# Two accumulators in place of three for the experts' rows, in a block of attention and 64 routed experts

## The reference, cut to what matters

```python
mod = (silu(c) @ wmod)                                # shifts, scales and gates of both halves
h = layernorm(x) * (1 + ca) + sa
x = x + ga * attention(h)                             # 8 batches of 512 tokens, 16 heads, band of +-64
h = layernorm(x) * (1 + cb) + sb
x = x + gb * experts(h)

def experts(h):                                       # n = 4096 tokens of width 256
    scores = sigmoid(h @ gate_w.T)                    # 64 experts
    topk_idx = 8 experts of each token, out of its 4 best groups of 8
    topk_w = scores[topk_idx] / sum * 2.5
    buf[e, pos] = h[token]                            # at most CAP = 256 tokens for each expert
    y = (silu(buf @ w_gate) * (buf @ w_up)) @ w_down  # width 128 in between
    out = zeros((n, 256)).at[token].add(y * topk_w)   # each token gets the sum of its experts' rows
```

## Time and profile before

| what | us |
|---|---|
| median of 3 runs | 974.45 (972.28 to 976.3) |
| the profiled execution | 980.85 |
| its span, first to last instruction | 979.1 |
| POOL's adding scatters (line 737), first start to last start | 696.06 to 937.31 |
| last rows landed, loads of the sums begin | 941.2 |
| VectorE's work on the sums | 946.73 to 976.0 |

### The profile page before, as it was taken

How to read it: one execution, slowest core, us unless ns; L and a number is a source line. 1 busy time by engine, 2 the same in 40 slices (tenths; PEclk the granted TensorE clock), 3 DMA queues, 4 the chain that set the end, 5 groups by cost and what they waited for, 6 DMA issues and landing times.

```text
span 979.1 us, 15496 instructions
## 1 busy us (share of the span) xinstructions
PE 728.8 (74%) x4789; PEld 477.4 (49%) x4816; DVE 509.6 (52%) x1976; ACT 402.7 (41%) x883; POOL 507.6 (52%) x514
## 2 busy tenths in 40 slices
PE   5679999989888988988987775200999988888200
PEld 3335556455454554554563443100888777676100
DVE  3176669678689678577676664500222221222038
ACT  3236665555555555565543341000444343433100
POOL 5000011256375474464555656776488888887730
PEclk9879999899999998998998976555999999999655
DMA  8684998366455464464344449201999998889877
GB/s 303 176 329 146 318 339 248 117 203 219 169 194 201 156 229 142 161 201 148 106 155 145 148 139 276 80 26 34 251 276 279 264 219 163 155 166 190 202 227 320
DMA packets 165262, 191.47 MB, mean 196 GB/s; under 512 B 21753, under 2 KB 146709, under 8 KB 165180
## 3 DMA queue, kind: packets, MB, share of 16 engines
q1 hardware_dynamic: 128764, 134.14, 42.8%
q0 software_dynamic: 30720, 38.03, 18.9%
q10 hardware_dynamic: 5696, 18.30, 4.9%
HBM read 100.64 MB, written 110.67 MB: 216 GB/s over the span
## 4 chain that ended last, share of the span: by engine, by line
PE 36%; DVE 21%; issue 14%; POOL 12%; DMA 10%; ACT 4%; another core or an unknown queue 1%; ACTq 1%; POOLq 0%; DVEq 0%; SPq 0%
DMA acc_d<-ys,xg 8%; POOL acc_d L737 6%; DVE junk L1297 5%; PE stageA L990 4%; POOL slots_d L661 4%; PE scores L1024 4%; PE outT L1066 4%; PE scoresT L1240 4%; PE stageA L1006 3%; PE scoresT L1046 3%; PE scoresT L1050 3%; PE stageC L1107 2%; DVE sc L1395 1%; PE turns L1076 1%; PE stageC L1125 1%
## 5 line engine op out<-in xcount | busy, mean ns | idle before, releaser
L661 POOL DMA_INDIRECT slots_d<-H,dest x256 | 257.8, 1007 | 206.3 <-PE outT L1066 73.6
L1297 DVE CUSTOM_DVE_ANT_0 junk<-scores,mask 128x256 bf16<-128x256 f32 x512 | 188.1, 420 | 102.3 <-PE scores L1024 58.1
L737 POOL DMA_INDIRECT acc_d<-ys,xg x128 | 198.2, 1548 | 60.3 <-issue 29.6
L798 ACT ACTIVATE PT<-scoresT 128x512 f32<-128x512 f32 (+1 forms) x320 | 154.2, 513 | 99.8 <-PE scoresT L1050 79.6
L1240 PE MATMUL scoresT<-xgT,wgu 128*128 128x256 f32 x512 | 127.8, 393 | 23.1 <-ACT xgT L903 23.1
L1046 PE MATMUL scoresT<-mask,identb 128*128 128x512 bf16 (+1 forms) x320 | 113.8, 356 | 17.1 <-ACT PT L798 9.9
L1240 PEld LDWEIGHTS scoresT<-xgT,wgu 128*128 128x128 f32 x512 | 96.0, 194 | 48.3 <-ACT xgT L903 35.1
L1024 PE MATMUL scores<-Ks,Qs 96*128 96x256 bf16 x512 | 103.2, 285 | 17.9 <-DVE mrowmax L1297 12.8
L1050 PE MATMUL scoresT<-Qs,Ks 98*128 98x256 bf16 (+1 forms) x640 | 113.8, 260 | 0.0
L1066 PE MATMUL outT<-PT,Va 128*32 128x256 f32 (+1 forms) x1280 | 91.5, 358 | 6.6 <-ACT parts L780 3.4
L1050 PEld LDWEIGHTS scoresT<-Qs,Ks 98*128 98x128 bf16 x640 | 65.5, 102 | 39.5 <-issue 10.0
(11 more groups left out here) (225 smaller groups left out, 1115.8 us busy)
## 6 DMA issues: line engine op xcount, KB each, us to landing
xg<-slots_d SPq DMA_DIRECT2D x64, 324.0 KB
slots_d<-blank ACTq DMA_DIRECT2D x26, 648.0 KB, 5.7
parts_d<-parts SPq DMA_DIRECT2D x32, 384.0 KB, 3.9
Qs<-parts_d SPq DMA_DIRECT2D x96, 128.0 KB
Ks<-parts_d SPq DMA_DIRECT2D x90, 128.0 KB
acc_d<-zero SPq DMA_DIRECT2D x32, 272.0 KB
wgu<-L_ffn_w_gate_dram SPq DMA_DIRECT2D x64, 128.0 KB
wgu<-L_ffn_w_up_dram SPq DMA_DIRECT2D x64, 128.0 KB
```

Of the source, the lines that this page charges most:

```text
L661: pool.indirect_dma_start(out=slots_d[:, :], in_=H2[bt.par][:, t, :], in_offset=None, out_offset=bass.IndirectOffsetOnAxis(ap=dest[bt.par] ...
L737: pool.indirect_dma_start(out=acc_d[ACC[e]][:, :], in_=ys[e % NY][:, h, :], in_offset=None, out_offset=bass.IndirectOffsetOnAxis(ap=xg[e % ...
L798: sc_.activation(PT[m % NPT][:, :, 0:w], src, ACT.Exp).then_inc(sems["exp"], 1)
L1297: ins = v.tensor_tensor_reduce(out=junk[:, i, :], in0=bS[n % 2][:, i * 2 * P:(i + 1) * 2 * P], in1=mask[:, edge, :], scale=1.0, scalar=TAK ...
```

## The change

The accumulators become two: `ACC[e] = e % 2` for all experts. With that, POOL's wait ahead of an expert names the one two before it for all experts from 2 on. What belongs to the third accumulator goes: its two fills in each batch, its early load into `f2` with SP's wait for expert 53, and one of three operations for each batch at the end. `fg` is no longer behind the `f2` loads.

```diff
-        ACC = [e % 3 if e < 54 else e % 2 for e in range(E)]
+        ACC = [e % 2 for e in range(E)]
...
-                for k in range(1, 3):
+                for k in range(1, 2):
                     for h in range(2):
...
-            def load_f2():
-                rows_added(sp, max(e for e in range(E) if ACC[e] == 2))
-                for b in range(B):
-                    sp.dma_start(f2[b][:], acc_d[2][b * S:(b + 1) * S, :].rearrange("(p t) d -> p t d", p=P)
-                                 ).then_inc(mo["f2_ld"], 16)
-
...
-                if e == E - 5:
-                    load_f2()
...
-            pool.wait_ge(s_zero, 16 * (4 * B + 1))
+            pool.wait_ge(s_zero, 16 * (2 * B + 1))
...
             dve.wait_ge(s_fg, 16)
-            dve.wait_ge(mo["f2_ld"], 16 * B)
             for b in range(B):
...
                 v.tensor_tensor(a[:, 0], a[:, 0], a[:, 1], ALU.add).then_inc(mo["fsum"], 1)
-                dve.wait_ge(mo["fsum"], 3 * b + 1)
-                v.tensor_tensor(a[:, 0], a[:, 0], f2[b][:], ALU.add).then_inc(mo["fsum"], 1)
-                dve.wait_ge(mo["fsum"], 3 * b + 2)
+                dve.wait_ge(mo["fsum"], 2 * b + 1)
                 v.tensor_tensor(a[:, 0], a[:, 0], fg[:, b, :].unsqueeze(1).to_broadcast([P, T, D]), ALU.mult
```

## The result

| | us |
|---|---|
| before, median of 4 runs | 973.47 (972.28 to 976.3) |
| changed, median of 4 runs | 990.74 (984.97 to 994.91) |
| ratio, changed to before | 1.0168, 95% interval 1.0134 to 1.0201 |
| profiled execution of the changed kernel | 984.97, span 983.2 |

The forecast was 977.3 us, with 967.5 to 984.5 as its range; the time lies outside it. Two later comparisons on other runs of both kernels gave 1.0149 (1.009 to 1.0209) and 1.0179 (1.0156 to 1.0202).

What follows compares the result with a forecast made beforehand. POOL's adding scatters were taken to bound the experts' half; +12.8 - 5.9 + 0.5 - 3.6 - 1.0 = +2.8 us, taking the median from 974.45 to 977.3 us, range 967.5 to 984.5.

Steps and rivals of the forecast that it cites:

- What bounds: Experts' half: POOL's 128 adding scatters are the limit, 1.85 us each, and a wait there has no slack.
- The threshold: Experts' half: a second scatter that lands within 4.81 us of its start is free; beyond it the excess is paid.
- The new wait, +12.8 us: Experts' half: POOL waits for expert e - 2, 26 experts wait, 12.8 us more in all.
- The table's rule: Expert e starts at the later of previous scatter + 1.85 and second scatter of e - 2 + landing time + 0.74.
- rival 1: Experts' half: landings under load are longer, 6.0 us in the first fifteen experts; total +8.7, 983.2 us; chance 0.25.
- Readings as they stand.: Experts' half: landing times read from the trace of before are used unchanged to price the wait with two accumulators.
- The early read, -5.9: Experts' half: without the eight loads of f2 and fg from 898 us, POOL's stalls from expert 56 on go, -5.9 us.
- `fg`, +0.5: Experts' half: fg's load alone, some 10 us earlier, lengthens one or two landings, +0.5 us, between 0 and 2.
- The end, -3.6: After the scatters: with two VectorE operations a batch, transfers at 410 GB/s become the limit, -3.6 us.
- rival 3: The end: VectorE's whole saving counts, -9.8 for -3.6, 971.1 us, countered by 410 GB/s as a ceiling; chance 0.06.
- The fills, -1.0: Attention half, first batch: fewer fill bytes shorten TensorE's 1.9 us wait for the maxima, -1.0 us, between 0 and -1.9.
- Rival 2: Experts' half: landings shorten to under 4.81 us as waiting spaces the scatters; total -10.0, 964.5 us; chance in full 0.13.

Runs made afterwards that it cites:

- wait_alone: The kernel before with three accumulators, only POOL's wait ahead of expert e names expert e - 2: 977.02 us against 955.83, ratio 1.0231.
- third_unread: The changed kernel with three accumulators and the waits of before, the third filled and added to but not read: 944.56 us against 955.83.
- paced: The kernel before, early read of the third accumulator spread: fg first, then one load after each landing of experts 53 to 60; 972.27 us against 973.5.
- shifted_before: The kernel before, SP's loads held back until TensorE has made gate and up of expert e + 5: 953.92 us against 955.48, ratio 0.9991.
- light_after: The changed kernel with the weights of experts 36 to 63 never loaded: 952.28 us, ratio to before 0.996.

## Why the prediction was wrong

**The direction of the balance was right, the size was not.** The parts, in its own order:

1. **What bounds** (POOL, 1.85 us for a scatter; a wait shows at once): right. Every microsecond of stall is in the result; `wait_alone` has +22.7 us of scatters and +21 us of time.
2. **The threshold** (5.55 - 0.74 = 4.81 us): right as far as it could be read. Expert 9 lands at 725.18 + 6.82 = 732.00, expert 11 starts at 732.74.
3. **The new wait, +12.8 us: this is the term that failed.** It measured 24 to 28 us: the changed kernel's three stretches of 259.1 to 263.4 us against 235.2 of the run with the same work and without the wait. The stalls ahead of experts 2 to 32 are 20.7 us in the first profile, where 8 to 18 were named. The table's rule held: fed with the changed kernel's own landings (3.81 from expert 54 on, as before) it gives 22.1, 24.5 and 26.9 us for the three profiles, whose stalls are 24.2, 26.3 and 28.5. What failed is what was put in.
   - *One reading for fifteen.* Experts 0 to 14 stood in the table with 5.30 us, the row of expert 12. The traces have their landings: 5.50 us on the mean in the first profile of before, 5.97 in the second, 5.63 and 5.53 in those of `third_unread` and `paced`. With all landings in place the table gives 15.6 us in the first profile and 17.8, 18.4 and 18.3 in the others. So 3 to 6 us were missing before any landing had moved, and the 5.6 us from which rival 1 was to decide lies among these means.
   - *"Readings as they stand."* The other 7 to 10 us, an estimate from the same sums, come from putting the landings of before into the new order. How much such a table hangs on the moments of the loads is seen in the control `shifted_before`, whose landings would give 25.7 us. They are not a property of the scatters. They depend on what else is released at the same moment, and that moves with the wait: a landing lets go SP's loads within 0.02 us and POOL's next scatter 0.74 us later. Before, a landing freed SP but POOL didn't wait for it; the scatters met the loads now here, now there, with 3.8 to 6.9 us and 5.5 on the mean. Now every second expert meets two bursts (6.0 us on the mean, up to 7.34), its neighbour few (4.8), and the maximum of each pair is paid. Among experts 2 to 30 the mean did not grow; only its distribution did the harm.
4. **The early read, -5.9**: right, 235.2 against 240.0 to 241.3 us of scatters.
5. **`fg`, +0.5**: too small, if what follows it is its own. It is issued at 904.18 in the changed profile, followed by [0.77] and [1.41] ahead of experts 54 and 55, 1.6 us over the usual 0.30; in the other two profiles these two stalls make 3.3 and 2.1 us. No run separates it, and the 24 to 28 us of the third term hold it already.
6. **The end, -3.6**: right, 38.0 to 38.4 in place of 41.3 to 41.8 us, bound by the transfers. The 410 GB/s that went in are a mean and no ceiling: slices of 3 us reach 419 GB/s before and 422 after, so rival 3's counter-argument was too strong, though the term came out.
7. **The fills, -1.0**: not to be told from 0. TensorE's wait for the maxima, 1.9 us in the earlier trace rows, is 0.5 us in the second profile of before and 0.5 and 0.9 in the two with the fills back; the changed kernel has 0 to 0.2. The place was right, but half of a wait of 0.5 to 0.9 us is less than 1.0.

With 26 us for the third and the fifth term together the sum would have been 26 - 5.9 - 3.6 - 1.0 = +15.5; measured were 13 to 17. Rival 1 (+8.7) came nearest. Its first form, longer landings of the unread fifteen, is in the traces and is the smaller part of the miss; the larger part is a mechanism that no rival named. Rival 2 named the spacing by waits as a help ("scatters no longer queue behind each other"); the same spacing lined them up with the loads. The wait is cheap only with the loads taken away, in `light_after`.

## What to carry to other kernels

A wait for a landing that today is hidden with a latency near its limit must not be priced with today's latencies: read the latency of every link, not of those that are easy to see, and ask what else the same landing sets off, for once the engine waits for it, its next transfer and those loads start together, round after round. If there is no way round such a wait, hold the loads back by a few microseconds; here three ways of doing so each gave back about half of the loss (0.7% in place of 1.5 to 1.8%) without moving a byte less. And compare the halves of a kernel between profiles, not the spans: 10 us of luck in the first half hid most of the loss in the second.

## What was not expected of the hardware

- A scatter of 128 rows of 1 KB lands 3.7 to 3.8 us after its issue began when little else moves, about 5.5 on a share of 1.1, and 6.2 to 7.3 when 1.4 MB of loads are issued together with it. Same transfer, same queue.
- VectorE's sum of 128x1024 floats took 1.22 us alone and 3.25 us beside a sum of the same size on GpSimd, which itself took 2.65 to 3.38 us.
- The first half of one and the same kernel differed by 29 us between two profiles (first scatter of before at 667.4 and at 696.1 us), with the stretch of scatters within 1.3 us. Most of it goes with the comparison, each of which ran on one chip (667 to 671 us in three, 688 to 690 in a fourth); whether the chip or the hour does it is open.
